# Attention scores on the two row halves of the array, and sixteen groups written out

## The chip, the cores and the metric

The kernel runs on one core of one Trainium2 chip. The metric is the device time of one execution in microseconds (us), the median of the runs shown. All times inside the program come from one profiled execution and are given from the start of its span.

## What is computed

Two layers on an input of 2 sequences x 1024 tokens x 512 features, each of the form x + s * silu(g), with s an attention and g a feed-forward part of the normalised x. The change touches the attention of the second layer alone:

```python
q = q * cos + _rotate_half(q) * sin          # 32 heads of 16
k = k * cos + _rotate_half(k) * sin          # 8 key/value heads
qg = q.reshape(b, HKV, G, t, DH)             # 4 query heads share one key head
scores = jnp.einsum('bhgtd,bhkd->bhgtk', qg, k) / math.sqrt(DH)
scores = jnp.where(causal[None, None, None], scores, jnp.finfo(jnp.float32).min)
attn = jax.nn.softmax(scores, axis=-1)
ctx = jnp.einsum('bhgtk,bhkd->bhgtd', attn, v)
```

## The kernel before

The attention stage handles 16 groups (2 sequences x 8 key heads), one after the other; a group is the 4 query heads that share a key head, over 1024 queries and 1024 keys. q and k lie in DRAM as three stacked parts of 16 rows (48 rows, PART), so that one matmul of 48 rows gives the score of one head at full precision.

Of each group two things are made on TensorE (PE).

**Items** (line 1594) only find the maximum of each query's scores. Queries are on the output partitions, keys along the row. There are 48 items a group, 12 for each head; their widths are 512 columns (24 times), 384, 256 and 128 (8 times each). An item goes to one of three spare PSUM banks, taken in turn. VectorE (DVE) reduces it (line 1535 with the causal mask, line 1538 for a first half without a mask) and so frees the bank (semaphore spare_free). When all maxima of a group are there, a small transpose (line 1601), a copy (line 1549) and two DMAs (line 1448) lay them as a row of the group's q tile (qst).

**Steps** make the scores again, with keys on the partitions, the maximum already subtracted (a row of -1 in the k tile kst against the row of maxima). A group has 24 steps (NC); a step is two matmuls of equal width (line 1612, one for each hh) into a pair of banks, and one exp on ScalarE (ACT, line 1515) over both. There are two such pairs, so step c waits for the exp of step c-2. Two steps make a unit of four heads; for each unit the weighed sum (line 1630) multiplies the values with the four heads' probabilities: four 32-column products, on the four column strips of the array, each in two records. GpSimd (POOL) masks the diagonal blocks (line 1483). Widths of the 12 units: 512 (six), 384, 256, 128 (two each). Twice a group the sums are copied, transposed on PE (line 1639) and divided on DVE (lines 1557, 1559).

The 48 items beside the steps of group n belong to group n+1 (items) and, after the maxima at step 19, to group n+2 (early items); items of the first group run alone, ahead of the steps. On PE each step's code is: two score matmuls, one item, the weighed sum (odd steps), then the other items. So between two weighed sums stand eight matmuls of the score kind: four items and four score matmuls.

The operands before: both q tile and k tile of a buffer hold 96 rows of data. Heads of even number use rows 0 to 47, odd ones rows 48 to 95, and the k tile exists twice, with zeros in the other half's rows. So every item has 96 rows and every score matmul 98 (two rows of maxima, M_ROW). Three buffers (STACKS) are cleared once by DVE (line 1523) and filled by SyncE's queue (SP), four DMAs a group (lines 1438 and 1440). PE's first item of a group waits for all of them (qk_in, LOADED).

The function groups() writes the code of each engine: group 0's first three steps (HEAD), then a hardware loop (line 1418) whose body is three groups and which runs four times, then groups 12 to 15 written out. All five engines run this loop.

Of the kernel before, what the change touches and what calls it, by code (L numbers as in the profile page):

```python
# [5 lines left out]
F32 = mybir.dt.float32  # L6
F32R = mybir.dt.float32r
# [6 lines left out]
P = 128  # L14
# [1273 lines left out]
M_ROW = 2 * PART  # L1288
# [6 lines left out]
ITEMS = [(h, q, at, min(CH, (q + 1) * P - at)) for h in range(HG) for q in range(QB) for at in range(0, (q + 1) * P, CH)]  # L1295
TURN_MAXIMA = 19
TURN_FIRST_HALF = 10
LOADED = 4 * 16
# [34 lines left out]
def layer1_attention(nc, ident_d, mask_d, fixed_d, q_scr, k_scr, v_all, ctx_sb):  # L1333
# [4 lines left out]
    with ExitStack() as ctx:  # L1338
# [7 lines left out]
        fixed = sb("fixed", [P, 2, 1])  # L1346
        qst = sb("qst", [P, STACKS, 2, T], F32R)
        kst = sb("kst", [P, STACKS, 2, T], F32R)
# [20 lines left out]
        ROUNDS = (NG - 1) // STACKS  # L1369

# [29 lines left out]
        def groups(eng, step, tail):  # L1400
# [15 lines left out]
            for c in range(HEAD):  # L1416
                run(c, 0, 0, True)
            with eng.Fori(0, ROUNDS - 1) as j:
                for k in range(STACKS):
                    for c in range(HEAD, NC):  # L1420
                        run(c, j, k)
                    for c in range(HEAD):
                        run(c, j, k + 1)
            for n in range((ROUNDS - 1) * STACKS, NG):
                for c in range(HEAD if n == (ROUNDS - 1) * STACKS else 0, NC):
                    run(c, 0, n)
# [5 lines left out]
        def _(sp):  # L1432
            def load(g):

                n, u, _ = g
                for par in range(2):
                    r = slice(par * PART, par * PART + PART)
                    sp.dma_start(kst[r, u, par].bitcast(F32), k_scr[bass.ds(n, 1)].rearrange("n c d t -> (n c d) t")).then_inc(qk_in[u], 16)
                    src = q_scr[bass.ds(n * HG, HG)].rearrange("(i p) c d t -> p (c d) i t", p=2)[par]
                    sp.dma_start(qst[r, u].bitcast(F32), src).then_inc(qk_in[u], 16)  # L1440

            def maxima(g, first=False):
# [4 lines left out]
                for par in range(2):  # L1447
                    sp.dma_start(qst[M_ROW + par:M_ROW + par + 1, u].rearrange("o i (b q) -> o (i b) q", q=P).bitcast(F32),
# [8 lines left out]
            sp.dma_start(fixed[:, :, :], fixed_d).then_inc(fixed_in, 16)  # L1457
            for u in range(STACKS):
                sp.wait_ge(cleared, u + 1)
                load(group(0, u))  # L1460
            maxima(group(0, 0), True)
            with sp.Fori(0, ROUNDS - 1) as j:
                for k in range(STACKS):
                    step(group(j, k), group(j, k + 1), group(j, k + STACKS))
            for k in range(STACKS):
# [437 lines left out]
```

## Time and profile before

| what | value |
|---|---|
| median of 3 runs | 1793.93 us (1789.36 to 1794.99) |
| span of the profiled execution | 1792.7 us |
| attention stage, first item to last operation | 1141.9 to 1717.9 us |
| PE busy, whole span | 1521.2 us (85%) |
| DVE busy, whole span | 1148.1 us (64%) |
| ACT busy, whole span | 607.1 us (34%) |
| mean granted clock of PE | 0.904 |

The profile lists, for each engine, when each instruction started and how long it took, and before an idle stretch what released it. PE's matmuls overlap with one another, so that the distance from one start to the next tells more than the duration. The granted clock is 1.00 at 2.4 GHz and 0.50 at 1.2 GHz. PEld is the weight load that goes ahead of each matmul.

### The profile page before, as it was taken

What the parts mean: (1) busy time and instruction counts of PE and PEld (TensorE: products, weight loads), DVE (VectorE), ACT (ScalarE), POOL (GpSimd) and SP (SyncE); (2) the same over time, 40 slices, a digit from 0 to 9 for tenths busy, and PEclk for the clock granted to TensorE, in tenths of its full rate; (3) what the DMA queues carried; (4) which work ended last, traced back from release to release, by engine and by line L of the source; (5) the groups of instructions that cost most, each with busy time, mean ns of one, the idle gap of its engine ahead of it and who ended that gap; (6) DMA issues with size and microseconds to landing.
All of it is one profiled execution on the core that took longest, in us unless ns stands there. A gap on an engine that the chain in (4) does not pass through costs nothing. (4 is left out here: it accounts for less than half of the span.)

```text
span 1792.7 us, 24031 instructions
## 1 busy us (share of the span) xinstructions
PE 1521.2 (85%) x7034; PEld 1036.6 (58%) x7034; DVE 1148.1 (64%) x2429; ACT 607.1 (34%) x859; POOL 340.2 (19%) x382
## 2 busy tenths in 40 slices
PE   0399889898846881999999999699999999999969
PEld 0366657566535660777777776355555555555447
DVE  5576875768645455455555543688687786888527
ACT  4224223242223330111111111046456465666632
POOL 2243343334312230000000000012122121121211
PEclk9988979889767895999999999579899898999979
DMA  7200000100023432100000000402112111211032
GB/s 263 94 1 1 24 24 1 47 1 24 1 89 125 150 124 89 30 25 18 24 25 18 15 9 0 87 8 48 28 27 54 27 27 27 54 27 29 2 131 82
DMA packets 48596, 84.12 MB, mean 47 GB/s; under 512 B 8899, under 2 KB 16657, under 8 KB 48506
## 3 DMA queue, kind: packets, MB, share of 16 engines
q1 hardware_dynamic: 41874, 78.13, 15.0%
q10 hardware_dynamic: 6632, 4.97, 0.9%
q8 instruction: 35, 0.57, 0.1%
q14 instruction: 55, 0.45, 0.1%
HBM read 58.54 MB, written 24.26 MB: 46 GB/s over the span
## 5 line engine op out<-in xcount | busy, mean ns | idle before, releaser
L1515 ACT ACTIVATE f_prob<-f_bank 128x1024 f32<-128x1024 f32 (+3 forms) x384 | 304.4, 811 | 216.6 <-PE f_bank L1612 214.5
L1594 PE MATMUL f_bank<-f_kst,f_qst 96*128 96x512 f32 (+3 forms) x768 | 282.8, 412 | 24.9 <-DMA f_qst<-q_scr 12.5
L1535 DVE CUSTOM_DVE_ANT_0 f_bank<-f_bank,f_mask 128x128 f32<-128x128 f32 (+3 forms) x512 | 248.5, 503 | 79.5 <-PE f_bank L1594 64.0
L1594 PEld LDWEIGHTS f_bank<-f_kst,f_qst 96*128 96x128 f32 x768 | 153.0, 204 | 181.0 <-DVE f_mx L1535 62.3
L1612 PE MATMUL f_bank<-f_qst,f_kst 98*128 98x512 f32 (+3 forms) x768 | 217.0, 367 | 1.2 <-ACT f_prob L1515 1.2
L1483 POOL TENSOR_SCALAR_AFFINE_SELECT f_prob<-f_prob 128x256 f32<-128x256 f32 x256 | 104.0, 407 | 467.8 <-ACT f_prob L1515 467.2
L1538 DVE TENSOR_REDUCE f_mx_first<-f_bank 128x1 f32<-128x512 f32 x256 | 176.1, 688 | 17.4 <-issue 8.1
L1630 PE MATMUL f_bank<-f_prob,f_vst 128*32 128x512 f32 (+3 forms) x1536 | 169.3, 514 | 1.0 <-ACT f_prob L1515 0.8
L37 PE MATMUL d_bank<-xtl,d_wgh 128*128 (+1 forms) x352 | 143.1, 407 | 8.9 <-DMA d_zz<-z_gu_scr 8.9
L1612 PEld LDWEIGHTS f_bank<-f_qst,f_kst 98*128 98x128 f32 x768 | 135.2, 199 | 20.6 <-ACT f_prob L1515 9.3
L1187 ACT ACTIVATE d_hs<-d_bank 128x512 f32<-128x512 f32 (+1 forms) x44 | 26.3, 598 | 348.8 <-PE d_bank L39 348.8
L39 PE MATMUL d_bank<-xth,d_wgh 128*128 (+1 forms) x352 | 140.4, 399 | 0.0
L38 PE MATMUL d_bank<-xth,d_wgl 128*128 (+1 forms) x352 | 139.6, 397 | 0.0
L546 DVE TENSOR_TENSOR al<-af,ah 128x512 fp32r<-128x512 f32 x48 | 65.1, 1356 | 90.7 <-ACT ah L416 90.7
L1137 DVE TENSOR_TENSOR d_hs<-d_hs,d_bank 128x512 f32<-128x512 f32 (+1 forms) x44 | 30.2, 687 | 133.5 <-ACT d_hs L1187 133.5
L370 POOL TENSOR_TENSOR pb<-at,qkv 128x2048 f32<-128x2048 f32 x16 | 94.5, 5906 | 87.2 <-ACT at L423 87.2
L358 POOL TENSOR_TENSOR pa<-qkv 128x2048 f32<-128x2048 f32 x16 | 72.9, 4554 | 199.1 <-DVE sc L450 142.4
L37 PE MATMUL bank<-w2l,ah 128*128 128x512 f32 x192 | 92.3, 481 | 12.8 <-DVE al L546 12.8
L415 ACT ACTIVATE af<-bank,b_sb 128x512 f32<-128x512 f32 x48 | 33.0, 687 | 197.1 <-PE bank L39 197.1
L1472 POOL COPY f_vst<-v_all 128x256 f32 (+1 forms) x16 | 6.3, 397 | 458.9 <-POOLq L1000 458.9
L37 PEld LDWEIGHTS d_bank<-xtl,d_wgh 128*128 128x128 f32 (+1 forms) x352 | 65.7, 187 | 34.9 <-issue 19.2
L39 PE MATMUL bank<-w2h,ah 128*128 128x512 f32 x192 | 84.3, 439 | 0.0
(225 smaller groups left out, 2761.6 us busy)
## 6 DMA issues: line engine op xcount, KB each, us to landing
f_qst<-q_scr SPq DMA_DIRECT2D x32, 384.0 KB, 6.1
q_scr<-c_qh SPq DMA_DIRECT2D x32, 256.0 KB
wst<-L_ffn_w SPq DMA_DIRECT2D x6, 1024.0 KB, 6.5
f_kst<-k_scr SPq DMA_DIRECT2D x32, 192.0 KB, 5.2
d_qw<-L_ffn_qweight_gu SPq DMA_DIRECT2D x40, 128.0 KB, 2.6
xall<-L_attn_x SPq DMA_DIRECT2D x2, 2048.0 KB, 16.2
xb<-L_attn_x SPq DMA_DIRECT2D x4, 1024.0 KB, 5.6
x_d<-xb SPq DMA_DIRECT2D x4, 1024.0 KB, 4.3
```

The lines of the kernel that those rows point to most:

```text
L37: pe.matmul(out, wh, ml, start=first, stop=False)
L38: pe.matmul(out, wl, mh, start=False, stop=False)
L39: return pe.matmul(out, wh, mh, start=False, stop=last)
L358: pool.tensor_tensor(pa[:, :, :, :], q, k, ALU.mult).then_inc(p1_done, 1)
L370: pool.tensor_tensor(pb[:, :, :, :], a, v, ALU.mult).then_inc(p2_done, 1)
L1483: pool.affine_select(out=p, in_=p, compare_op=ALU.is_ge, fill=0.0, base=0, pattern=[[0, 2], [1, P]], channel_multiplier=-1).then_inc(maske ...
L1515: act.activation(prob[:, c // 2 % 2, c % 2 * 2:c % 2 * 2 + 2, lo:], score_bank[c % 2][:, :, lo:], ACT.Exp, scale=D ** -0.5).then_inc(exp_d ...
L1535: dve.tensor_tensor_reduce(sc, sc, mask[:, CH - w:CH], 1.0, LEAST, ALU.add, ALU.max, mx[:, u, h % 2, h // 2, q:q + 1]).then_inc(spare_free, 1)
L1538: dve.tensor_reduce(mx_first[:, h % 2, h // 2, q:q + 1], sc, AX.X, ALU.max).then_inc(spare_free, 1)
L1594: pe.matmul(spare[v][:, 0:w], qst[0:M_ROW, u, h // 2, q * P:q * P + P], kst[0:M_ROW, u, h % 2, at:at + w], start=True, stop=True).then_inc ...
L1612: mm = pe.matmul(score_bank[c % 2][:, hh, lo:], kst[0:M_ROW + 2, u, hh, k * P:k * P + P], qst[0:M_ROW + 2, u, c % 2, h * CH + lo:(h + 1) * ...
L1630: mm = pe.matmul(sum_bank[2 * D * hh:2 * D * (hh + 1), lo:], vst[:, u, k], prob[:, i % 2, hh, lo:], start=(k == 0), stop=(k == last))
```

## The change

Three things are altered.

1. Every item and every score matmul uses 64 rows of the array: even heads rows 0 to 63, odd heads rows 64 to 127 (half_rows). Of these 48 hold data, one (row 48 of the half) holds the maxima against -1, and 15 are zero. The k tile is no longer kept twice. While items run, the row of maxima has to be zero, so each load of a group has two more DMAs that write zeros there; LOADED rises from four to six DMAs.
2. Items are put in another order: items of an even and an odd head alternate, with equal widths next to one another. Counts and widths are the same.
3. The hardware loop is gone: all 16 groups are written out on every engine.

At the start DVE clears two tiles for each buffer, and SP's first load waits until all three buffers are cleared rather than the first.

```diff
-M_ROW = 2 * PART
+HALF_ROWS = P // 2
...
-ITEMS = [(h, q, at, min(CH, (q + 1) * P - at)) for h in range(HG) for q in range(QB) for at in range(0, (q + 1) * P, CH)]
+ITEMS = [(2 * i + par, q, at, min(CH, (q + 1) * P - at)) for i in range(HG // 2) for q in range(QB)
+         for at in range(0, (q + 1) * P, CH) for par in range(2)]
+def stack_rows(par):
+    return slice(par * HALF_ROWS, par * HALF_ROWS + PART)
+def half_rows(par):
+    return slice(par * HALF_ROWS, (par + 1) * HALF_ROWS)
...
-LOADED = 4 * 16
+LOADED = 6 * 16
...
-            for c in range(HEAD):
-                run(c, 0, 0, True)
-            with eng.Fori(0, ROUNDS - 1) as j:
-                for k in range(STACKS):
-                    for c in range(HEAD, NC):
-                        run(c, j, k)
-                    for c in range(HEAD):
-                        run(c, j, k + 1)
-            for n in range((ROUNDS - 1) * STACKS, NG):
-                for c in range(HEAD if n == (ROUNDS - 1) * STACKS else 0, NC):
-                    run(c, 0, n)
+            for n in range(NG):
+                for c in range(NC):
+                    run(c, 0, n, n == 0 and c < HEAD)
...
-                    r = slice(par * PART, par * PART + PART)
-                    sp.dma_start(kst[r, u, par].bitcast(F32), k_scr[bass.ds(n, 1)].rearrange("n c d t -> (n c d) t")).then_inc(qk_in[u], 16)
+                    r = stack_rows(par)
+                    sp.dma_start(kst[r, u].bitcast(F32), k_scr[bass.ds(n, 1)].rearrange("n c d t -> (n c d) t")).then_inc(qk_in[u], 16)
...
+                    row = par * HALF_ROWS + PART
+                    sp.dma_start(qst[row:row + 1, u].bitcast(F32), kst[P - 1:P, 0:HG // 2].bitcast(F32)).then_inc(qk_in[u], 16)
...
-                sp.wait_ge(cleared, u + 1)
+                sp.wait_ge(cleared, STACKS)
...
-                dve.tensor_copy(kst[:, u], fixed[:, :, :].broadcast_to([P, 2, T])).then_inc(cleared, 1)
+                dve.tensor_scalar(qst[:, u], fixed[:, :].broadcast_to([P, HG // 2 * T]).rearrange("p (i t) -> p i t", t=T), 0.0, None, ALU.mult)
+                dve.tensor_copy(kst[:, u], fixed[:, :].broadcast_to([P, T])).then_inc(cleared, 1)
...
-                pe.matmul(spare[v][:, 0:w], qst[0:M_ROW, u, h // 2, q * P:q * P + P],
-                          kst[0:M_ROW, u, h % 2, at:at + w], start=True, stop=True).then_inc(spare_ps, 1)
+                r = half_rows(h % 2)
+                pe.matmul(spare[v][:, 0:w], qst[r, u, h // 2, q * P:q * P + P], kst[r, u, at:at + w],
+                          start=True, stop=True).then_inc(spare_ps, 1)
...
-                    mm = pe.matmul(score_bank[c % 2][:, hh, lo:], kst[0:M_ROW + 2, u, hh, k * P:k * P + P],
-                                   qst[0:M_ROW + 2, u, c % 2, h * CH + lo:(h + 1) * CH], start=True, stop=True)
+                    r = half_rows(hh)
+                    mm = pe.matmul(score_bank[c % 2][:, hh, lo:], kst[r, u, k * P:k * P + P],
+                                   qst[r, u, c % 2, h * CH + lo:(h + 1) * CH], start=True, stop=True)
```

In group 0, PE's code before enters the loop after step 2; f_bank is PSUM, L1612 are score matmuls, L1594 items, L1630 the weighed sum, ISA and REGISTER_ALU the reckoning of wait values that the loop's counter calls for.

```order
L1418 UNCONDITIONAL_BRANCH
L1418 ISA
L1612 MATMUL f_bank<-f_qst,f_kst 128x384 x2
L1593 ISA
L1594 MATMUL f_bank<-f_kst,f_qst 128x512
L1623 ISA
L1625 REGISTER_ALU
L1627 ISA
L1630 MATMUL f_bank<-f_prob,f_vst 32x512 x4
L1593 REGISTER_ALU
L1594 MATMUL f_bank<-f_kst,f_qst 128x128
```

PE at the same place after the change; L1617 are score matmuls, L1598 items, L1635 the weighed sum.

```order
L1617 MATMUL f_bank<-f_qst,f_kst 128x384 x2
L1598 MATMUL f_bank<-f_kst,f_qst 128x512
L1635 MATMUL f_bank<-f_prob,f_vst 32x512 x4
L1598 MATMUL f_bank<-f_kst,f_qst 128x384
L1617 MATMUL f_bank<-f_qst,f_kst 128x256 x2
L1598 MATMUL f_bank<-f_kst,f_qst 128x384
L1617 MATMUL f_bank<-f_qst,f_kst 128x256 x2
L1598 MATMUL f_bank<-f_kst,f_qst 128x512
L1635 MATMUL f_bank<-f_prob,f_vst 32x384 x4
```

The branch into the loop and the reckoning are gone, and two items of one width now stand next to one another in the sequence of items. Which of the two row halves a matmul takes is not in these rows: score matmuls take the lower rows, then the upper; items alternate.

SP's queue at the start of the stage, before (one buffer and the beginning of the next):

```order
L1431 UNCONDITIONAL_BRANCH
L1457 DMA f_fixed<-fixed_d 128x2
L1438 DMA f_kst<-k_scr 48x1024
L1440 DMA f_qst<-q_scr 48x2x1024
L1438 DMA f_kst<-k_scr 48x1024
```

and after:

```order
L1433 UNCONDITIONAL_BRANCH
L1462 DMA f_fixed<-fixed_d 128x1
L1440 DMA f_kst<-k_scr 48x1024
L1442 DMA f_qst<-q_scr 48x2x1024
L1444 DMA f_qst<-f_kst 1x16x128
L1440 DMA f_kst<-k_scr 48x1024
```

Each half has a third DMA, of one row, behind its two.

DVE at the start of the stage, before (ISA is the reduction of line 1535, in two parts):

```order
L1519 UNCONDITIONAL_BRANCH
L1523 CAST f_kst<-f_fixed 128x2048 x3
L1535 ISA f_bank,f_mx<-f_bank,f_mask 128x128
L1535 ISA f_mx 128x1
L1535 ISA f_bank,f_mx<-f_bank,f_mask 128x256
```

and after:

```order
L1525 TENSOR_SCALAR f_qst<-f_fixed 128x2048
L1526 CAST f_kst<-f_fixed 128x1024
L1525 TENSOR_SCALAR f_qst<-f_fixed 128x2048
L1526 CAST f_kst<-f_fixed 128x1024
L1525 TENSOR_SCALAR f_qst<-f_fixed 128x2048
L1526 CAST f_kst<-f_fixed 128x1024
```

Three clears of 2048 elements a partition have become three of 2048 and three of 1024, all of them ahead of the first load.

## Rows read from the trace of the kernel before

**Rows 1.** The page: span; busy us, share and instructions of DVE.
```profile
span 1792.7 us, 24031 instructions
...
PE 1521.2 (85%) x7034; PEld 1036.6 (58%) x7034; DVE 1148.1 (64%) x2429; ACT 607.1 (34%) x859; POOL 340.2 (19%) x382
```
**Rows 2.** Busy us (instructions) of each engine, granted clock; two groups, maxima to maxima.
```profile
1554.90:1619.50 64.60, 63.77 (x403) 36.29 (x404) 54.38 (x172) 39.96 (x53) 13.70 (x34) 1.00 0.17 38
```
**Rows 3.** Timeline, PE: start, us; the small transpose, one a group at step 19.
```profile
1202.76 0.28 PE L1601 MATMUL f_bank<-f_ident,f_mx 128*32 128x128 f32 x1 [0.28 <-DVE f_mx L1543]
...
1267.20 0.28 PE L1601 MATMUL f_bank<-f_ident,f_mx 128*32 128x128 f32 x1 [0.28 <-DVE f_mx L1543]
...
1310.00 0.28 PE L1601 MATMUL f_bank<-f_ident,f_mx 128*32 128x128 f32 x1 [0.28 <-DVE f_mx L1543]
...
1374.45 0.28 PE L1601 MATMUL f_bank<-f_ident,f_mx 128*32 128x128 f32 x1 [0.28 <-DVE f_mx L1543]
...
1416.31 0.28 PE L1601 MATMUL f_bank<-f_ident,f_mx 128*32 128x128 f32 x1 [0.28 <-DVE f_mx L1543]
...
1480.78 0.28 PE L1601 MATMUL f_bank<-f_ident,f_mx 128*32 128x128 f32 x1 [0.28 <-DVE f_mx L1543]
...
1522.68 0.28 PE L1601 MATMUL f_bank<-f_ident,f_mx 128*32 128x128 f32 x1 [0.28 <-DVE f_mx L1543]
...
1619.49 0.27 PE L1601 MATMUL f_bank<-f_ident,f_mx 128*32 128x128 f32 x1 [0.37 <-DVE f_mx L1543]
```
**Rows 4.** A loop end: DVE's timeline, then windows as in Rows 2.
```profile
1282.29 0.69 DVE L1538 TENSOR_REDUCE f_mx_first<-f_bank 128x1 f32<-128x512 f32 x1 [2.66 <-issue]
...
1285.00:1290.00 5.00, 5.00 (x25) 2.72 (x25) 3.47 (x10) 0.77 (x2) 0.71 (x3) 0.50 0.01 2
...
1300.00:1305.00 5.00, 5.00 (x36) 2.91 (x32) 3.63 (x14) 2.82 (x4) 1.28 (x4) 1.00 0.00 0
```
**Rows 5.** Timeline of PE between loop ends, full clock.
```profile
1411.67 0.39 PE L1612 MATMUL f_bank<-f_qst,f_kst 98*128 98x128 f32 x2
1411.89 0.57 PE L1594 MATMUL f_bank<-f_kst,f_qst 96*128 96x512 f32 x2
...
1423.61 0.63 PE L1612 MATMUL f_bank<-f_qst,f_kst 98*128 98x512 f32 x2
1424.08 0.23 PE L1594 MATMUL f_bank<-f_kst,f_qst 96*128 96x128 f32 x1
1424.24 1.07 PE L1630 MATMUL f_bank<-f_prob,f_vst 128*32 128x512 f32 x8
1425.23 0.39 PE L1594 MATMUL f_bank<-f_kst,f_qst 96*128 96x256 f32 x1
```
**Rows 6.** DVE's waits in the stretch of Rows 2: total us, times, longest.
```profile
DVE f_bank L1535 <- PE f_bank L1594: 6.8, 13, 0.7
...
DVE f_mx_first L1538 <- PE f_bank L1594: 0.5, 2, 0.2
```
**Rows 7.** Window of DVE alone: the 48 items ahead of the first steps.
```profile
1142.60:1169.10 26.50, 25.09 (x81) 0.50 0.39 74
```
**Rows 8.** The last group, which has no items beside it: window, PE's timeline.
```profile
1689.00:1694.00 5.00, 4.34 (x28) 1.62 (x27) 0.68 (x2) 4.08 (x6) 1.22 (x3) 1.00 0.00 0
...
1686.37 1.43 PE L1612 MATMUL f_bank<-f_qst,f_kst 98*128 98x512 f32 x4
...
1688.72 1.20 PE L1612 MATMUL f_bank<-f_qst,f_kst 98*128 98x512 f32 x4
```
**Rows 9.** Start of the stage: timeline; last a group by form, xcount, busy, mean ns.
```profile
1132.46 3.50 DVE L1523 CAST f_kst<-f_fixed 128x2048 fp32r<-128x2048 f32 x3 [2.13 <-DMA f_fixed<-fixed_d]
1133.72 0.34 SPq L1438 DMA_DIRECT2D f_kst<-k_scr  x1
...
1141.95 0.45 PE L1594 MATMUL f_bank<-f_kst,f_qst 96*128 96x128 f32 x1 [12.46 <-DMA f_qst<-q_scr]
...
L1121 DVE TENSOR_SCALAR d_wq<-d_qw,lane_shift 128x512 uint32<-128x512 uint32 x30 | 14.4, 481 | 1.9 <-DMA d_qw<-L_ffn_qweight_gu 1.8
```

More of the change, by code:

```diff
@@ L1345, in layer1_attention @@
         ident, mask = sb("ident", [P, P]), sb("mask", [P, CH])
-        fixed = sb("fixed", [P, 2, 1])
-        qst = sb("qst", [P, STACKS, 2, T], F32R)
-        kst = sb("kst", [P, STACKS, 2, T], F32R)
+        fixed = sb("fixed", [P, 1])
+        qst = sb("qst", [P, STACKS, HG // 2, T], F32R)
+        kst = sb("kst", [P, STACKS, T], F32R)
         vst = sb("vst", [P, STACKS, QB, 2 * D])
@@ L1368, in layer1_attention @@
         NI = len(ITEMS)
-        ROUNDS = (NG - 1) // STACKS
         def span(h, k):
@@ L1447, in maxima @@
                 for par in range(2):
-                    sp.dma_start(qst[M_ROW + par:M_ROW + par + 1, u].rearrange("o i (b q) -> o (i b) q", q=P).bitcast(F32),
+                    row = par * HALF_ROWS + PART
+                    sp.dma_start(qst[row:row + 1, u].rearrange("o i (b q) -> o (i b) q", q=P).bitcast(F32),
                                  mt[par * 2 * QB:(par + 1) * 2 * QB, u].bitcast(F32)).then_inc(m_in[u], 16)
@@ L1455, in step @@
                     load(third)
-            sp.dma_start(fixed[:, :, :], fixed_d).then_inc(fixed_in, 16)
+            sp.dma_start(fixed[:, :], fixed_d).then_inc(fixed_in, 16)
             for u in range(STACKS):
-                sp.wait_ge(cleared, u + 1)
+                sp.wait_ge(cleared, STACKS)
                 load(group(0, u))
             maxima(group(0, 0), True)
[L1462 to L1465, printed above, removed]
-                step(group(ROUNDS - 1, k), group(ROUNDS - 1, k + 1), group(ROUNDS - 1, k + STACKS) if k == 0 else None)
+            for n in range(NG - 1):
+                step(group(0, n), group(0, n + 1), group(0, n + STACKS) if n + STACKS < NG else None)
         @block.gpsimd
@@ L1882, in shape_constants @@
     c["mask_d"] = mask
-    fixed = np.zeros((P, 2, 1), f)
-    fixed[M_ROW, 0], fixed[M_ROW + 1, 1] = -1, -1
+    fixed = np.zeros((P, 1), f)
+    fixed[PART], fixed[HALF_ROWS + PART] = -1, -1
     c["fixed_d"] = fixed
```

## The prediction

> **What bounds the kernel now.** I read the page first, only to place the change: the profiled span is 1792.7 us [rows 1], 1.2 below the median of 1793.93, so I work in this span and add 1.2 at the end. The change touches the attention stage alone (1142 to 1718 us), so everything else is left as it is.
>
> Within the stage I read the rows that mark one point of every group. From 1522.68 to 1619.49, three groups, each takes 32.27 us; from 1202.76 to 1267.20, two groups, each takes 32.22 [rows 3]. The first stretch lies in groups that are already written out, the second in the loop: code in a line or in the loop's body runs at the same pace. At three places a group takes longer: 1267.20 to 1310.00 is 42.80, 1374.45 to 1416.31 is 41.86, 1480.78 to 1522.68 is 41.90 [rows 3]. These are the three jumps back of the loop (four passes).
>
> What bounds a group? In the windows of two groups PE is busy 63.77 of 64.60 us, DVE 54.38, ACT 39.96, at a granted clock of 1.00 [rows 2]. Busy PE alone proves nothing, so I look at the starts: two score matmuls of 512 columns take 0.47 us to the next matmul, two of 128 columns 0.22, and a weighed sum of 512 columns 0.99 [rows 5]. These fit back-to-back work. DVE, in the same two groups, waits for PE's items 6.8 + 0.5 us [rows 6]. So PE sets the pace and DVE stands close behind: without those waits DVE would need 32.27 - 3.65 = 28.6 us a group. This is the number on which the size of the gain hangs.
>
> **The loop's end.** There DVE waits 2.66 us for nothing that the profile shows ("issue"), which I take for the fetch of code after the jump. PE, which needs DVE to free a bank, stands still. Afterwards the clock is 0.50 at 1285 and back at 1.00 at 1300; in five us PE does 25 matmuls at the one and 36 at the other [rows 4]. Stall and slow clock together cost 42.80 - 32.25 = 10.6, then 9.6 and 9.7: 29.9 us. With no jump all of it goes, if straight code keeps up, and the written-out groups of today show that it does at 32.27. Bounds: -29.9, and 0 if something of the kind comes back.
>
> **PE's work in a group.** 96 matmuls of the score kind: 48 of 512 columns at 0.47 / 2 = 0.235, 16 of 128 at 0.11, and, between these, 16 of 384 at about 0.18 and 16 of 256 at about 0.13: 11.3 + 1.8 + 2.9 + 2.1 = 18.1 us. Weighed sums and transposes are the other 14. Nothing in this trace shows two row halves at work at once. The nearest row is the weighed sum: eight records of 512 columns on four column strips pass in 0.99 us, where one after the other at 0.235 they would need 1.9 even with one pass each [rows 5]. Strips of columns do run side by side. For rows I bound the gain from 0 (no overlap) to one half (9 us a group).
>
> Half isn't reached, for two reasons. First the order: score matmuls come as lower, upper; four items stand between two weighed sums, and their halves alternate. The written-out code gives lower item, (lower, upper) scores, upper item, lower item, (lower, upper) scores, upper item. In order, with neighbours on different halves side by side, these are five slots for eight matmuls. Second the weight loads: two matmuls of 128 columns need 0.22, no less than a load each, and I assume that loads are not doubled: 96 x 0.11 = 10.6 us at least. Five eighths of 18.1 is 11.3, so both say about 11.3, and PE needs 32.25 - 6.8 = 25.5 us a group.
>
> **Two rules of the skill at this place.** The trace already pays for each passage between a score matmul and a weighed sum, since 128 and 32 output columns alternate 24 times a group and the weighed sum's 0.99 has the passage back in it [rows 5]. The Trainium skill (TensorEngine Tiling (Array Packing), "Key Properties") says that a change of tiling mode drains the engine; by it the 24 passages stay 24, and only the transposes and the small one gain edges, six a group. [...] The same skill (TensorE: Matmul & The Clock Gate, "The mechanism") says that matmuls on different row strips run concurrently; by that PE would gain the half of the bound above, and the sum would not change, since DVE's floor comes first. No row here shows either.
>
> **What is late next.** DVE, at 28.6. A second way to the same number: ahead of the first steps DVE takes 48 items alone in 26.5 us, busy 25.09, although PE is at clock 0.50 [rows 7]. In a full group it is busy 54.38 / 2 = 27.2, so 2.1 more for maxima and divisions: 26.5 + 2.1 = 28.6. ACT isn't the bound: in the last group, with no items, two wide steps and a weighed sum take 1688.72 - 1686.37 = 2.35 us [rows 8], and wide units are half of 12; 28 is not reached by that chain.
>
> Can DVE be kept at work without a gap? PE is in a weighed sum for 0.99 us, with a matmul of 0.4 behind it, and the passage: about 1.6 to 1.7 us in which no new item is ready. Three banks hold 3 x 26.5 / 48 = 1.65 us of DVE's work. This is just enough for items of mean size and too little where two narrow ones stand together, which the new order makes common. I give it 0.08 us for each of 12 units, 1.0 us. Group: 28.6 + 1.0 = 29.6, against 32.25: -2.65. It counts for the 15 groups that have items beside them: **-39.7**. Ends: 28.6 (-55) and 32.25 (0).
>
> **Last group.** It has no items and PE and ACT hand over to one another. Pairs save up to 0.47 of a unit's 2.35, but two exps of a pair already fill 2.0 of it (ACT is busy 4.08 of 5 in the window) [rows 8]. So 0.25 for wide units, less for others: -2 us (0 to -4).
>
> **Start of the stage.** SP's loads of group 0 start at 1133.72, behind the first clear of 1.22 us; the first item starts at 1141.95, when the last of them has landed [rows 9]. Now all six clears come first. A copy of 2048 costs 1.2 (3.50 for three); one of 1024 costs then about 0.7; a tensor_scalar of 2048 is not in the trace, it lies between 1.2 and four times that of 512 elements, 4 x 0.48 = 1.9 [rows 9]. I take 1.3, near the copy. Three times 2.0 is 6.0, so the loads start 4.7 us later (up to 6.5). The one-row DMA between group 0's loads adds an issue of some 0.4 ahead of its last large one, and another behind it. Sum **+5.3** (5 to 8): nothing covers it, PE stands idle there today. In later groups the two more issues on SP, 0.8 us, come with a load that is needed 18 steps later, over 20 us, and SP's next duty, the maxima, is as far off: nothing.
>
> The first items, 26.5 us, are DVE's and remain. No wait values reckoned by registers: 0, since written-out groups are no faster today [rows 3].
>
> **Sum.** 1792.7 - 29.9 - 39.7 - 2 + 5.3 = 1726.4; with 1.2 added, **1728 us** (1727.6).
>
> **Rivals.**
> Straight code isn't free: with 16 groups in a line on five engines the fetch stalls now and then, and the idle time drops the clock as at the loop's end. Against it: groups 12 to 15, at 32.27. Its price is the 29.9 given back: about 1758.
> The halves don't overlap, or drains eat it: only loop and start remain, 1793.9 - 29.9 + 5.3 = 1769. For it: no row shows overlap by rows. Against it: the column strips.
> PE beyond DVE's floor is impossible by my count; should clear, last group and starvation all come out at their good ends, 1793.9 - 29.9 - 55 - 4 + 5 = 1710.
> **Slower**: PE, no longer the bound, idles while it waits for DVE's banks, and the clock falls to 0.50 in mid-group. At the loop's end 17 us at half clock cost 10.6 - 2.7 = 7.9, so 9.1 us of work took 17: 1.87 times as long. PE's 25.5 become 48 us, 18 more than 29.6. The gain of 66 is gone when 3.6 of 16 groups' time is at half clock; with half of them it is 1728 + 8 x 18.1 = 1873. For it: the first items ran at 0.50 throughout [rows 7]. Against it: the last group, where PE has no items at all, keeps 1.00 [rows 8], and a PE at half clock would be the bound again, and so without gaps.
>
> **How the numbers follow.** DVE-bound group with the loop gone (1712 to 1745): 0.62. Stalls in straight code (1745 to 1760): 0.10. Little or no overlap (1755 to 1772): 0.14. Beyond the good end: 0.04. Clock falls: 0.07 slower, 0.03 about equal. That leaves 1706 to 1769 for 8 in 10. A measurement of this kernel tells 0.3%, 5 us, from no change. Faster 0.90, same 0.03, slower 0.07.
>
> **What would show it.** Marks of groups 29 to 30 us apart, evenly, with no 42; no "issue" wait over 2 us on DVE; pairs of 512 columns under 0.35 us; DVE's waits for items near 1 us a group and PE's weight loads waiting for DVE instead; first item near 1147. Wrong would be: marks at 32.2 (no overlap), clock 0.50 between 1200 and 1700, or marks under 28.6.

## The result, and the profile after

The changed kernel takes **1766.32 us** (median of 4 runs, 1761.45 to 1767.31) against 1794.38 for the kernel before, run beside it. The ratio is 0.9838, 95% interval 0.9818 to 0.9858: 28 us faster. I had forecast 1728 with a range of 1706 to 1769. The sign is right and the time lies inside the range, near its upper end, but the gain forecast was 66 us and the one measured is 28.

The page of the changed kernel, span and busy times:

```profile
span 1759.7 us, 21845 instructions
...
PE 1444.5 (82%) x7034; PEld 940.3 (53%) x7034; DVE 1140.1 (65%) x2432; ACT 600.2 (34%) x859; POOL 339.6 (19%) x382
```

The two profiled spans differ by 33 us, the medians by 28. The stage begins 5.2 us earlier in this execution (first DMA of the stage issued at 1125.37, before at 1130.60), in code that the change doesn't touch. Over all the profiled runs below that point lies between 1124.2 and 1132.7, although none of their edits touches the code ahead of it. So I compare stretches within the stage, and two medians a few us apart prove little.

The marks of the groups, on PE's timeline (start, us; line 1605 is the small transpose, once a group), to be read against [rows 3]:

```profile
1203.00 0.40 PE L1605 MATMUL f_bank<-f_ident,f_mx 128*32 128x128 f32 x1 [0.49 <-DVE f_mx L1538]
...
1235.16 0.28 PE L1605 MATMUL f_bank<-f_ident,f_mx 128*32 128x128 f32 x1 [0.49 <-DVE f_mx L1538]
1266.16 0.28 PE L1605 MATMUL f_bank<-f_ident,f_mx 128*32 128x128 f32 x1 [0.49 <-DVE f_mx L1538]
1298.61 0.40 PE L1605 MATMUL f_bank<-f_ident,f_mx 128*32 128x128 f32 x1 [0.49 <-DVE f_mx L1538]
...
1364.59 0.28 PE L1605 MATMUL f_bank<-f_ident,f_mx 128*32 128x128 f32 x1 [0.49 <-DVE f_mx L1538]
1395.52 0.28 PE L1605 MATMUL f_bank<-f_ident,f_mx 128*32 128x128 f32 x1 [0.49 <-DVE f_mx L1538]
1457.40 0.28 PE L1605 MATMUL f_bank<-f_ident,f_mx 128*32 128x128 f32 x1 [0.49 <-DVE f_mx L1538]
...
1649.86 0.37 PE L1605 MATMUL f_bank<-f_ident,f_mx 128*32 128x128 f32 x1 [1.54 <-DVE f_mx L1546]
```

No group takes 42 us any more. But they are uneven: 1364.59 to 1395.52 is 30.9, two groups to 1457.40 are 30.9 each, 1266.16 to 1298.61 is 32.45. From 1203.00 to 1649.86 it is 14 groups at 31.92 on average. In the kernel before, less the three loop ends, it was 32.2. So a group has become 0.3 us shorter, where I had forecast 2.65, and even the groups of 30.94, in which the clock keeps its level, are only 1.3 us shorter.

Windows of the changed kernel (busy us and instructions of PE, PEld, DVE, ACT, POOL, then granted clock): two even groups as in [rows 2], then three stretches around 1267:

```profile
1395.52:1457.40 61.88, 54.98 (x402) 24.84 (x402) 53.49 (x173) 39.21 (x52) 13.59 (x34) 1.00 0.23 41
1264.20:1267.60 3.40, 2.60 (x23) 1.41 (x27) 2.75 (x15) 1.60 (x3) 0.00 (x0) 1.00 0.00 0
1267.60:1271.00 3.40, 3.40 (x15) 1.17 (x7) 2.01 (x9) 1.88 (x3) 0.00 (x0) 0.50 0.05 10
1271.00:1274.40 3.40, 2.90 (x22) 1.25 (x25) 2.75 (x9) 2.65 (x4) 0.30 (x1) 1.00 0.83 164
```

PE now has 3.45 us a group in which it does nothing (61.88 less 54.98, by two), where it had 0.4. And there are short falls of the clock to 0.50: nine stretches from 1200 to 1650, each of which begins between 0.4 us ahead of a mark and 1.4 behind it. The mark stands behind steps 12 to 17, which are narrow (384, 256, 128 columns). In such a stretch PE gets 15 matmuls through instead of 22 or 23. Eight of the 14 groups have a fall, and they take 31.8 to 33.7 us instead of 30.9.

DVE's waits and those of PE's weight loads in the same two even groups (total us, times, longest), to be read against [rows 6]:

```profile
DVE f_bank L1538 <- PE f_bank L1598: 5.7, 15, 0.5
...
DVE f_mx_first L1541 <- PE f_bank L1598: 1.0, 2, 0.7
```
```profile
PEld f_bank L1598 <- DVE f_mx_first L1541: 10.6, 19, 0.8
PEld f_bank L1598 <- DVE f_mx L1538: 10.0, 20, 0.8
```

DVE still waits 3.35 us a group for items, before 3.65. At the same time PE's items wait for DVE. In a group of 30.94 us PE is idle for 3.45 us and DVE for 4.2 (61.88 less 53.49, by two), so neither is the bound alone: each runs dry in turn. This is the core of the miss.

The overlap by row halves is there. On PE's timeline, one weighed sum to the next:

```profile
1398.33 0.50 PE L1617 MATMUL f_bank<-f_qst,f_kst 64*128 64x512 f32 x2
1398.66 0.39 PE L1598 MATMUL f_bank<-f_kst,f_qst 64*128 64x512 f32 x1
1398.98 1.07 PE L1635 MATMUL f_bank<-f_prob,f_vst 128*32 128x512 f32 x8
1399.98 0.50 PE L1598 MATMUL f_bank<-f_kst,f_qst 64*128 64x512 f32 x2
```

Two score matmuls of 512 columns take 0.33 us to the next start, before 0.47 [rows 5]. It isn't the 0.235 of full overlap. That the halves overlap, and that 64 rows aren't just quicker than 96, shows a run described below (halves_old_order), in which neighbours among the items often lie on one half:

```profile
1401.82 0.62 PE L1597 MATMUL f_bank<-f_kst,f_qst 64*128 64x512 f32 x2
1402.28 0.39 PE L1616 MATMUL f_bank<-f_qst,f_kst 64*128 64x512 f32 x1
```

These two items of 512 columns take 0.46 us to the next start, as two of 98 rows do (0.47).

From the last item to the weighed sum it is 0.32, and the weighed sum's 1.00 is what it was. What has become dearer is the way from a transpose back to a score matmul. Behind the small transposes at 1267.20 [rows 3] and, after the change, at 1395.52 (above) stand:

```profile
1267.28 0.73 PE L1612 MATMUL f_bank<-f_qst,f_kst 98*128 98x512 f32 x2
```
```profile
1395.74 0.49 PE L1617 MATMUL f_bank<-f_qst,f_kst 64*128 64x512 f32 x2
```

From start to start it is 0.22 us instead of 0.08. With the two groups of other transposes, each 0.17 dearer (0.20 instead of 0.03), that is some 0.5 us of PE a group. What the way into the transposes costs can't be told from the wait for a bank.

The start of the stage (SP's queue, DVE), to be read against [rows 9]:

```profile
1125.37 0.36 SPq L1462 DMA_DIRECT2D f_fixed<-fixed_d  x1
1127.50 1.23 DVE L1525 TENSOR_SCALAR f_qst<-f_fixed 128x2048 fp32r<-128x2048 f32 x1 [2.40 <-DMA f_fixed<-fixed_d]
1128.65 0.69 DVE L1526 CAST f_kst<-f_fixed 128x1024 fp32r<-128x1024 f32 x1
...
1132.84 0.34 SPq L1440 DMA_DIRECT2D f_kst<-k_scr  x1
...
1142.83 0.77 PE L1598 MATMUL f_bank<-f_kst,f_qst 64*128 64x128 f32 x3 [18.58 <-DMA f_qst<-f_kst]
```

The first DMA of the stage before:

```profile
1130.60 0.36 SPq L1457 DMA_DIRECT2D f_fixed<-fixed_d  x1
```

From the first DMA to the first item it was 1141.95 - 1130.60 = 11.35 us and is 1142.83 - 1125.37 = 17.5: +6.1. The loads start 4.35 us later after that first DMA, and from the first load to the first item it is 9.99 us instead of 8.23.

### The profile page after: what moved, and what is told of

Read it like the earlier page. It is cut to its first block and busy times, and to the rows that moved or that the text cites. A ratio compares the mean times of both kernels' runs of the same rounds, so it can differ in the third digit from the quotient of the medians.

```text
span 1759.7 us, 21845 instructions
## 1 busy us (share of the span) xinstructions
PE 1444.5 (82%) x7034; PEld 940.3 (53%) x7034; DVE 1140.1 (65%) x2432; ACT 600.2 (34%) x859; POOL 339.6 (19%) x382
## 5 line engine op out<-in xcount | busy, mean ns | idle before, releaser
L1517 ACT ACTIVATE f_prob<-f_bank 128x1024 f32<-128x1024 f32 (+3 forms) x384 | 298.7, 810 | 190.8 <-PE f_bank L1617 190.8
L1598 PE MATMUL f_bank<-f_kst,f_qst 64*128 64x512 f32 (+3 forms) x768 | 268.7, 430 | 49.5 <-DMA f_qst<-f_kst 18.6
L1538 DVE CUSTOM_DVE_ANT_0 f_bank<-f_bank,f_mask 128x128 f32<-128x128 f32 (+3 forms) x512 | 239.8, 517 | 67.7 <-PE f_bank L1598 54.4
L1598 PEld LDWEIGHTS f_bank<-f_kst,f_qst 64*128 64x128 f32 x768 | 136.9, 198 | 225.4 <-DVE f_mx_first L1541 91.9
L1617 PE MATMUL f_bank<-f_qst,f_kst 64*128 64x512 f32 (+3 forms) x768 | 205.2, 405 | 2.7 <-ACT f_prob L1517 2.5
L1541 DVE TENSOR_REDUCE f_mx_first<-f_bank 128x1 f32<-128x512 f32 x256 | 168.4, 685 | 16.2 <-PE f_bank L1598 13.0
L1635 PE MATMUL f_bank<-f_prob,f_vst 128*32 128x512 f32 (+3 forms) x1536 | 173.1, 524 | 1.7 <-ACT f_prob L1517 1.3
L1617 PEld LDWEIGHTS f_bank<-f_qst,f_kst 64*128 64x128 f32 x768 | 98.1, 194 | 24.6 <-ACT f_prob L1517 17.9
L1474 POOL COPY f_vst<-v_all 128x256 f32<-128x256 f32 x16 | 6.3, 397 | 458.7 <-POOLq L1000 458.7
```

What stands on the lines that cost most here:

```text
L1517: act.activation(prob[:, c // 2 % 2, c % 2 * 2:c % 2 * 2 + 2, lo:], score_bank[c % 2][:, :, lo:], ACT.Exp, scale=D ** -0.5).then_inc(exp_d ...
L1538: dve.tensor_tensor_reduce(sc, sc, mask[:, CH - w:CH], 1.0, LEAST, ALU.add, ALU.max, mx[:, u, h % 2, h // 2, q:q + 1]).then_inc(spare_free, 1)
L1541: dve.tensor_reduce(mx_first[:, h % 2, h // 2, q:q + 1], sc, AX.X, ALU.max).then_inc(spare_free, 1)
L1598: pe.matmul(spare[v][:, 0:w], qst[r, u, h // 2, q * P:q * P + P], kst[r, u, at:at + w], start=True, stop=True).then_inc(spare_ps, 1)
L1617: mm = pe.matmul(score_bank[c % 2][:, hh, lo:], kst[r, u, k * P:k * P + P], qst[r, u, c % 2, h * CH + lo:(h + 1) * CH], start=True, stop=True)
L1635: mm = pe.matmul(sum_bank[2 * D * hh:2 * D * (hh + 1), lo:], vst[:, u, k], prob[:, i % 2, hh, lo:], start=(k == 0), stop=(k == last))
```

## Taking the change apart

My theory, once the result was known: the loop's end is worth what I said; row halves save little because DVE, and now the clock, take it back. Rivals: row halves don't overlap at all; straight code costs something; the order of the items, which I had charged with 1 us a group, does more.

**Written out, and nothing else (flat_only).** The kernel before with the loop replaced by the written-out form:

```diff
...
-            with eng.Fori(0, ROUNDS - 1) as j:
...
+            for n in range(NG):
+                for c in range(NC):
+                    run(c, 0, n, n == 0 and c < HEAD)
```

> The kernel before with nothing changed but the loop: all 16 groups written out, score matmuls as before on 98 and 96 rows. Theory (the loop's end cost 29.9 us and straight code is free): 1794.4 - 29.9 = 1764.5 us, marks of groups 32.2 us apart throughout. Rival (row halves carry a real part of the 28 us gained): above 1772. Rival (straight code costs something): marks uneven, over 32.3.

Measured 1758.09 us (1753.74 to 1760.90), ratio 0.9802 (0.9775 to 0.9829). Windows of two groups:

```profile
1387.60:1451.40 63.80, 62.96 (x404) 36.27 (x404) 54.57 (x172) 39.84 (x53) 13.69 (x34) 1.00 0.19 39
```

A group takes 31.9 us, evenly, at clock 1.00, with PE busy 31.5. The loop gave 36 us; straight code costs nothing, and even takes 0.3 off each group. Alone it is 8 us faster than the whole change: all four of its runs lie below all four of the change, though the intervals of the two ratios just overlap. The groups are as long in both, 31.95 us on average against 31.92. From its first DMA to its last operation the stage takes 552.8 us here and 559.0 in the changed kernel, and the 6 us between them are the later start. So the row halves with their order of items gain nothing in the groups, and lose at the start.

**Row halves and order, in the loop (halves_loop).** The changed kernel with the loop put back (the diff above, reversed, with the changed kernel's items, rows and loads).

> The changed kernel with the hardware loop put back: row halves, alternating items, six loads. Theory (row halves are worth about nothing once the later start is paid: +5.8 for the start, -1.3 a group in undisturbed groups, some of it given back by a clock that dips): 1790 to 1797 us. Rival (they are worth 20 us or more): under 1775.

Measured 1802.18 (1789.01 to 1811.34), ratio 1.0044 (1.0012 to 1.0076). Ten runs lie from 1789 to 1811, wider than those of any other kernel here but one_half. The same sign from the other side: everything but the loop costs some 8 us in either form. It even exceeds what I expected. In its profile the three groups with a jump back take 41.15, 44.66 and 43.21 us, so the loop's ends are back.

**All on one half (one_half).** All items and score matmuls use the lower 64 rows, so that the odd heads' results are left out:

```diff
-                r = half_rows(h % 2)
+                r = half_rows(0)
...
-                    r = half_rows(hh)
+                    r = half_rows(0)
```

> The changed kernel with every item and score matmul on the lower 64 rows (odd heads are left out, even heads are computed twice), so that none can overlap by rows. Theory (matmuls on different halves do run side by side, and that is what takes a group from 32.2 to 30.9): marks 32.2 to 32.4 us apart, clock 1.00 throughout, 1766 + 14 x 0.3 + 0 = 1768 to 1775 us. Rival (no overlap, the gain is from the order of items): marks at 30.9 as in the changed kernel.

Measured 2140.24 us (2126.58 to 2144.69 in three runs, 2551.15 in the fourth), ratio 1.1879. A large miss, from a cause that I hadn't in mind. Window:

```profile
1450.00:1550.00 100.00, 100.00 (x350) 53.32 (x353) 52.27 (x153) 37.08 (x46) 11.74 (x30) 0.50 0.14 25
```

PE is busy without a gap, and the granted clock is 0.50 (1.2 GHz), for 939 us on end; groups are 56.4 us apart. The kernel before, whose items and score matmuls use 96 and 98 rows, went from 0.50 to 1.00 at 1184, and the changed kernel, with 64 rows on both halves in turn, at 1182, both within the first group. So it isn't gaps on PE alone that hold the clock down: a PE that works all the time on 64 rows stayed at the low level too. As a test of overlap this run is void, since the clock is another; what it suggests is that matmuls on one half alone keep the clock down, and no other run puts that to the test. The evidence for overlap lies in the distances from start to start above: 0.33 us for two matmuls of 512 columns on two halves, 0.46 on one.

**DVE's work cut (dve_less, flat_dve_less).** Items are reduced over half of their columns (the maxima of the other half are left out), in the changed kernel and in the written-out kernel of before.

```diff
-dve.tensor_tensor_reduce(sc, sc, mask[:, CH - w:CH], 1.0, LEAST, ALU.add, ALU.max,
+dve.tensor_tensor_reduce(sc[:, 0:w // 2], sc[:, 0:w // 2], mask[:, CH - w:CH - w // 2], 1.0, LEAST, ALU.add, ALU.max,
...
-dve.tensor_reduce(mx_first[:, h % 2, h // 2, q:q + 1], sc, AX.X, ALU.max)
+dve.tensor_reduce(mx_first[:, h % 2, h // 2, q:q + 1], sc[:, 0:w // 2], AX.X, ALU.max)
```

> The changed kernel with every item reduced over the first half of its columns only (the maxima of the other half are left out), which takes some 9 us a group from DVE. Theory (in a clean group PE and DVE take turns in waiting for one another, DVE's time counts): groups of 27 us or less where the clock is full. Rival (PE and ACT alone set 30.9): marks unchanged.

> The same cut of DVE's reductions in the kernel before with all groups written out and nothing else changed. Theory (there PE is the bound, 31.9 us a group with 31.4 busy): marks 31 to 31.9 apart, hardly changed. Rival (DVE counts there too): under 30.

Measured 1705.12 and 1739.34 us, one run each. Windows of two groups, first with row halves, then without:

```profile
1399.10:1455.40 56.30, 51.97 (x402) 23.74 (x402) 35.54 (x173) 38.86 (x53) 13.56 (x34) 1.00 0.26 44
```
```profile
1382.80:1444.30 61.50, 61.34 (x404) 35.82 (x404) 38.27 (x172) 39.65 (x53) 13.69 (x34) 1.00 0.20 41
```

With a third of DVE's work gone a group takes 28.15 us with row halves and 30.8 without. With row halves and DVE at full work it is 30.9, so DVE costs 2.8 us a group there, and only 1.1 in the written-out kernel, where PE is busy 61.34 of 61.50 when DVE is cut. My expectation of 27 us or less for the first was too good.

What do the row halves save on PE itself? The two kernels differ by 2.6 us a group, where I had forecast 6.8. But in the first PE is still idle for 2.2 us a group (56.30 less 51.97, by two), and it has the new order of items, the second the old one. PE's busy time falls from 30.7 to 26.0, by 4.7 us. So the saving on PE is less than forecast, from 2.6 to 4.7 us; these two runs don't tell more.

## What the order of the items does

**Order alone, without row halves (pairs_flat).** The written-out kernel of before with the change's ITEMS.

> The kernel before, all groups written out, with nothing else but the changed kernel's order of items (even and odd head in turn). Theory (the order alone is worth nothing on 96 rows, so what is left against the written-out kernel of before comes from the row halves): within 4 us of 1758, clock 1.00 from 1180 us on. Rival (two narrow items next to one another starve DVE and cost a part of the 8 us by which the changed kernel is behind): 1762 or more.

Measured 1785.99 us (1780.56 to 1791.54), ratio 0.9959 (0.9927 to 0.9991). My theory fell: without row halves the order costs 28 us against flat_only. Window of two groups, and DVE's waits in it:

```profile
1401.70:1469.20 67.50, 64.33 (x402) 36.19 (x402) 54.91 (x173) 39.69 (x52) 13.67 (x34) 1.00 0.18 37
```
```profile
DVE f_bank L1525 <- PE f_bank L1584: 7.6, 16, 0.8
DVE f_mx_first L1528 <- PE f_bank L1584: 2.8, 6, 0.7
```

33.75 us a group instead of 31.9, at full clock. DVE waits for items 5.2 us a group; with the old order it was 3.6 (6.7 + 0.5 in two groups). The same work, in another order.

**Old order, with row halves (halves_old_order).** The changed kernel with the ITEMS line of before.

> The changed kernel with the items in the order of before (all items of one head, then of the next), so that items next to one another lie on the same half. Theory (the pairs of score matmuls bring what overlap there is worth, the items' order little): clean marks 30.9 to 31.4 apart, 1762 to 1772 us. Rival (items overlap in pairs and that counts): marks over 31.5, over 1772.

Measured 1754.43 us (1750.97 to 1760.78), ratio 0.9787 (0.9758 to 0.9816): 12 us better than the changed kernel.

```profile
1396.20:1457.00 60.80, 58.53 (x402) 28.66 (x402) 53.13 (x172) 38.93 (x52) 13.69 (x34) 1.00 0.24 41
```

Even groups are 30.4 us, and the clock falls only twice between 1200 and 1640 after the start. PE is busy 58.5 of 60.8: less overlap, as neighbours often lie on one half, and fewer gaps. With this order the row halves are worth 31.95 - 30.67 = 1.3 us a group on average against flat_only, 18 us over 14 groups; the start takes 6 of them, the group up to the second mark, most of which still runs at half clock, takes 37.0 instead of 33.1 and so another 4. That leaves 8, and from its first DMA to its last operation the stage takes 544.0 us against 552.8. The medians show only 4 (1758.1 against 1754.4); in the profiled run the stage begins 5.7 us later than in that of flat_only.

Why is the order so dear? The rule beside() deals items to steps by their widths. With the old order it gives exactly two items to each of the 24 steps, such as (128, 256), (384, 512), (512, 128). With the new one it gives one, two or three: (384), (512, 512), (512, 512), (128, 128, 256). Two explanations were open, the number in a step or equal widths in a row.

**Two in every step (two_a_step).** The changed kernel with

```diff
-    cost = [w + 96 for *_, w in ITEMS]
-    upto = lambda x: sum(sum(cost[:s + 1]) <= sum(cost) * x / NC + 1e-6 for s in range(len(ITEMS)))
     at = (c - TURN_MAXIMA) % NC
-    return range(upto(at), upto(at + 1))
+    return range(2 * at, 2 * at + 2)
```

> The changed kernel with two items in every step, in the same order of items (pairs of one width, even and odd head), where it has one to three by a reckoning of widths. Theory (a step with three items or one is what hurts, since PE then stands before DVE's banks with score matmuls behind it): clean marks 30.4, few falls of the clock, 1752 to 1757 us. Rival (items of one width in a row are what hurts: two of 512 hold DVE 1.4 us, two of 128 leave it dry): no better than 1764.

Measured 1770.23 us (1767.07 to 1772.27), ratio 0.9868 (0.9841 to 0.9895). Even groups take 31.7 us.

```profile
1404.00:1467.50 63.50, 55.99 (x402) 25.73 (x403) 53.86 (x172) 38.78 (x52) 13.57 (x34) 1.00 0.24 39
```

The number in a step isn't it. With equal widths in a row the even dealing is no better: even groups of 31.7 us instead of 30.9, although the intervals of the two ratios overlap.

**Wide beside narrow, on different halves (mixed_early).** Two items a step, one from an even head and one from an odd head whose sequence of widths is shifted by three; the clears early (below).

```diff
...
+TURNED = OF_HEAD[3:] + OF_HEAD[:3]
+ITEMS = [(2 * i + par, *(OF_HEAD, TURNED)[par][s]) for i in range(HG // 2) for s in range(len(OF_HEAD)) for par in range(2)]
...
```

> The same early clears, two items a step, one from an even head and one from an odd head whose sequence of widths is shifted by three, so that neighbours lie on different halves and wide stands beside narrow. Theory (row halves pay if the order keeps DVE fed): marks 29.5 to 30.2, 1740 to 1750 us. Rival (PE's passages and DVE's time leave nothing more): 30.4, 1752 or more.

Measured 1776.83 us (1774.11 to 1778.11), ratio 0.9913 (0.9888 to 0.9937).

```profile
1406.50:1438.10 31.60, 28.04 (x201) 12.55 (x201) 26.70 (x86) 19.44 (x26) 6.75 (x17) 1.00 0.24 40
```

31.6 us in an even group, slower than the old order's 30.4, although no two items of one step lie on one half. So equal widths in a row aren't the whole cause either. What the slow orders share is that even and odd heads take turns; what the old one has is its own particular succession of widths. Which of these counts stays open.

**Odd heads ahead of even ones (upper_first).** The changed kernel with the two halves swapped in ITEMS. The succession of widths stays as it is; between two weighed sums upper and lower matmuls now alternate without a break, so that by the reckoning of the prediction eight matmuls need four slots instead of five:

```diff
-          for at in range(0, (q + 1) * P, CH) for par in range(2)]
+          for at in range(0, (q + 1) * P, CH) for par in (1, 0)]
```

> The changed kernel with items in the order upper half, lower half, so that between two weighed sums upper and lower matmuls alternate without a break (four slots for eight instead of five). Theory (PE's time in score matmuls isn't what bounds a clean group): clean marks 30.6 to 31.0 apart, clock falls as often or oftener, 1762 to 1772 us. Rival (pairing bounds it): clean marks under 30, under 1755 us.

Measured 1764.51 us (1758.22 to 1769.33), ratio 0.9839 (0.9793 to 0.9884), the same as the changed kernel's 0.9838; the mean group is 31.91 us against 31.92, and the even groups take 30.9 in both. So the number of slots on PE isn't what bounds a group.

**The other item placed ahead of the weighed sum (items_first).**

```diff
-                run(todo[:1])
+                run(todo)
...
-                run(todo[1:])
```

> The changed kernel with PE's order in odd steps altered: both items ahead of the weighed sum, where today one of them stands behind it. Theory (DVE runs dry during the weighed sum since the third bank, free by then, is filled only after it): DVE's waits for items fall from 3.4 us a group to under 1.5, marks 29 to 30 us apart, about 1740 us. Rival (the waits come from elsewhere, or PE now stands before the weighed sum waiting for DVE and ACT is late): marks at 30.9 or above, 1766 or more.

Measured 1841.68 us (1839.46 to 1843.32), ratio 1.0269 (1.0249 to 1.0288). The window and two waits in it:

```profile
1470.90:1507.50 36.60, 33.37 (x202) 14.68 (x202) 27.10 (x87) 19.48 (x26) 6.78 (x17) 0.81 0.20 34
```
```profile
DVE f_bank L1538 <- PE f_bank L1598: 8.0, 11, 1.7
...
PEld f_bank L1617 <- ACT f_prob L1517: 4.4, 8, 0.8
```

DVE waits longer than before, 8 us in one group, not less. PE now stands before the weighed sum until DVE has freed a bank, and everything behind it is late; in turn PE idles and the clock is 0.81 on average. The rival was right, and more strongly than it said. How much of the 75 us is the waiting and how much the clock, this run doesn't tell apart. One item ahead of the weighed sum and one behind is much the better place.

## The falls of the clock, and the start

**Narrow score matmuls made twice (filler, and early_loads and filler_wide with the clears early).** In steps 12 to 17, or in all narrow steps for filler_wide, the two score matmuls are issued a second time.

```diff
+                if 12 <= c < 18:
+                    for hh in range(2):
+                        r = half_rows(hh)
+                        mm = pe.matmul(score_bank[c % 2][:, hh, lo:], kst[r, u, k * P:k * P + P],
+                                       qst[r, u, c % 2, h * CH + lo:(h + 1) * CH], start=True, stop=True)
```

> The changed kernel with the two score matmuls of steps 12 to 17 (the narrow ones ahead of the maxima) made twice, with the same result. Theory (the clock falls behind those steps because so little of the array is at work there, and each fall costs about 1.5 us a group): no fall of the clock between 1200 and 1650 us, marks 30.9 to 31.3 apart, 1766 - 10 = 1756 us. Rival (the falls have another cause): the same falls and 1766 or more.

Measured 1760.54 us (1752.06 to 1762.76), ratio 0.9816 (0.9766 to 0.9866), against 0.9838 for the changed kernel; the intervals overlap. In its profile there are three falls between 1200 and 1620 instead of eight, 11 of 14 groups take 31.0 to 31.4 us, and the mean group is 31.34 instead of 31.92:

```profile
1305.20:1367.30 62.10, 56.10 (x427) 26.29 (x427) 53.49 (x173) 39.22 (x52) 13.66 (x34) 1.00 0.23 41
```

Six more matmul pairs a group lengthen it by no more than 0.1 us. Whether they keep the clock up isn't shown: early_loads, which has the same doubling and differs from filler only in its start, had seven falls in the same stretch of its profiled execution. The cause of the falls stays open, and so does the gain in time.

**The clears.** First the three k tiles, then a q tile and its load:

```diff
-                sp.wait_ge(cleared, STACKS)
+                sp.wait_ge(cleared, u + 1)
...
+                dve.tensor_copy(kst[:, u], fixed[:, :].broadcast_to([P, T]))
+            for u in range(STACKS):
+                dve.tensor_scalar(qst[:, u], ..., 0.0, None, ALU.mult).then_inc(cleared, 1)
```

> The changed kernel with the doubled narrow score matmuls of steps 12 to 17 and with the clears in another order: the three k tiles first, then a q tile and at once its load. The first load then waits 3 x 0.69 + 1.22 = 3.3 us of clears rather than 5.7. Theory (the start's delay is the clears and is on the path): 2.4 us less than the kernel with doubled matmuls alone, about 1758 us. Rival (the landing of the loads doesn't follow their issue, since twelve large transfers share the DMA engines): no gain.

> The same, with the score matmuls of all narrow steps doubled (those of steps 2 to 7 too). Theory (the falls of the clock left over come from the narrow steps of the first half): no fall between 1200 and 1620 us, marks 31.0, 2 to 4 us less than with steps 12 to 17 alone. Rival (the extra matmuls now lengthen the groups): marks 31.3 or more, no gain.

> The changed kernel with the items' order of before and the clears in the order k tiles first. Theory (the clears are on the path): 2.4 us less than with the items' order alone, about 1752 us. Rival (the first item waits for the share of DMA, not for the issue): no gain, 1754.

Measured: early_loads 1756.85 us (1754.95 to 1758.56), ratio 0.9796 (0.9775 to 0.9816); filler_wide 1764.70 (1763.85 to 1768.01), ratio 0.9843 (0.9822 to 0.9864); old_order_early 1755.75 (1746.21 to 1760.19), ratio 0.9801 (0.9772 to 0.9830). The start of early_loads:

```profile
1124.23 0.36 SPq L1462 DMA_DIRECT2D f_fixed<-fixed_d  x1
1126.35 1.90 DVE L1525 CAST f_kst<-f_fixed 128x1024 fp32r<-128x1024 f32 x3 [2.39 <-DMA f_fixed<-fixed_d]
...
1129.41 0.34 SPq L1440 DMA_DIRECT2D f_kst<-k_scr  x1
...
1139.73 0.76 PE L1599 MATMUL f_bank<-f_kst,f_qst 64*128 64x128 f32 x3 [16.62 <-DMA f_qst<-f_kst]
```

From the first DMA to the first item it is 15.5 us instead of 17.5, and 14.8 in old_order_early: the clears are on the path, and 2 to 2.7 us come back. In the medians it doesn't stand out: early_loads is 3.7 us below filler, old_order_early 1.3 above halves_old_order, and the four runs of old_order_early alone spread over 14 us. Doubling all narrow steps went too far: even groups 31.4 us, and five falls stay between 1200 and 1620.

Among the kernels that leave no work out halves_old_order has the lowest median, 1754.4; flat_only with 1758.1, old_order_early and early_loads can't be told from it. All beat the kernel before; halves_old_order beats the change by 12 us, and their intervals don't overlap; flat_only beats it by 8.

## Why the prediction was right or wrong

**The loop.** Right, and a little short. Forecast -29.9. flat_only: 36 in the medians; in its profile the 14 groups between the second and the last mark take 447.2 us against 480.9, so -33.7, of which 29.9 are the three ends and the rest is 0.3 a group. I had argued from written-out groups at 32.27 that registers cost nothing; with all groups written out a group is 31.9, and where the 0.3 comes from I haven't tried. Against the forecast of nothing for the registers that is some 4 us of luck.

**The step that failed: "What is late next", group 29.6.** The sum took PE's need (25.5) and DVE's (28.6), said that the larger one holds, and added 1.0 for DVE running dry. In the change as it stands the mean group is 31.92, so instead of -39.7 for 15 groups there came 0.3 us for each of 14, and that much came in flat_only too, without row halves. So the term for the groups was nothing in the change as it stands. Its parts:
- The floor of DVE was read from its waits, as if these went away when PE is faster, but for 1.0 us. They went from 3.65 to 3.35 a group only. Reckoned in the same way, DVE's need is now 30.94 - 3.35 = 27.6, a little less than the 28.6 of the forecast, and still a group takes 30.94. PE and DVE wait for one another in turn: a third of DVE's work less shortens the group by 2.8, and in the old order row halves shorten it by 1.3. "The larger one holds" was the wrong rule for the two. That the three banks between them are what ties them together is read from the waits; no run had another number of banks.
- PE's saving, 6.8 us a group, was too high: it is 2.6 to 4.7 (dve_less). A pair of 512 takes 0.33, not 0.235, and the ways out of the transposes cost 0.5 more. But upper_first shows that fewer slots wouldn't have helped.
- The order of items was given at most 1.0 us a group ("too little where two narrow ones stand together"). The place was right and the size wrong: it costs 1.8 without row halves, and 1.25 with them (31.92 against 30.67), the latter with the falls of the clock in it.
- The falls of the clock were a rival with 0.07 on the slow side (and 0.03 about equal). They come, in the mild form of one short stretch in most groups, 1.0 us a group on average (31.92 against 30.9). Each lasts only some 3 to 7 us, so the price of that rival, 18 us a group, was never near. I had argued that the last group keeps 1.00; in the changed kernel even that group has a fall, at 1667.

**No overlap, 1769.** This rival gave nearly the measured time, by a wrong mechanism: the overlap exists, its gain went to order, clock and hand-over. That the time still fell into the range is luck: the range reached up to 1769 for this rival, and not for groups that stay as long as they are in the written-out kernel.

**The start.** Forecast +5.3, measured +6.1. The tensor_scalar cost 1.22, for which I had taken 1.3 with an upper end of 1.9. The clears came to 4.35 of it, forecast 4.7; the rest, 1.8 us, lies between the first load and the first item, where I had put 0.6.

**The last group.** Forecast -2. From the last mark to the end of the stage it was 34.2 us and is 34.5: nothing. The pairs are shorter there, but the falls at 1650 and 1667 lie in it.

**Sum by what was measured:** -33.7 for loop and straight code, -0.4 for the 14 groups against flat_only, -0.7 for the group ahead of them (33.6 to 32.9), +6.1 for the start, +0.3 at the end: -28.4, and 28 was measured.

## What to carry to other kernels

Where two engines near the same load hand over through a few banks, the time of both together is neither's own: measure it by cutting one engine's work, and don't take its waits as a gain to be had. Undo each part of a change alone; here one part gave 36 us and the rest took 8 back. The order of small items may be worth more than a faster engine: 12 and 28 us here. No rule for a good order came out of these runs (a steady mix of wide and narrow, mixed_early, was slower than the old order), so an order that works is worth keeping when other things change.

## What the runs showed of the hardware

A PE that was busy all the time (100.00 of 100.00 us), with all its items and score matmuls on the lower 64 rows, stayed at 1.2 GHz through the stage (granted clock 0.50 over 939 us), where the kernels with 96 and 98 rows, or with 64 rows on both halves in turn, rise to 2.4 GHz in their first group. Matmuls on different halves of the rows overlap in part: two of 512 columns pass in 0.33 us, against 0.47 one after the other on 96 or 98 rows and 0.46 on one half of 64. From a transpose of 128 rows to a matmul of 64 rows it took 0.20 to 0.22 us from start to start, to one of 98 rows 0.03 to 0.08. A hardware loop of this size lost about 10 us at each jump back, on a page that shows it only as "issue" and as a clock at half.
